# Attention and expert layer on one Trainium2 core: the batch loop in four groups of two pairs of heads, and another passage to the token tiles

## The reference

```
q = norm(x) @ Wq + bq;  k, v = ctx[:, :256] @ Wk + bk, @ Wv + bv     16 heads of 64
a = softmax(where(key > query, -1e30, q k^T / 8)) v @ Wo + bo
x = x + tanh(g_xattn) * a      (blind rows take the mean of all 1601 context rows instead)
e = argmax(norm(x) @ Wr + br)                                       one of 8 experts
x = x + tanh(g_ffn) * (relu(norm(x) @ W1[e] + b1[e]) @ W2[e] + b2[e] + what the other experts give on zero input)
```

## Time and profile before

| what | value |
|---|---|
| median of 3 executions | 360.89 us (360.82 to 364.35) |
| profiled execution, its span | 365.85 us, 363.8 us |
| granted TensorE clock, mean | 0.998 |
| PE / PEld busy | 345.6 / 283.3 us (95% / 78%) |
| DVE / ACT / POOL busy | 270.9 / 255.5 / 191.0 us (74% / 70% / 52%) |
| start and batch 0 / loop / batch 7 and tiles | 60.7 / 213.0 / 90.3 us |

### The profile page before, as it was taken

How to read it: one execution, slowest core, us unless ns; L and a number is a source line. 1 busy time by engine, 2 the same in 40 slices (tenths; PEclk the granted TensorE clock), 3 DMA queues, 4 the chain that set the end, 5 groups by cost and what they waited for, 6 DMA issues and landing times.

```text
span 363.8 us, 11160 instructions
## 1 busy us (share of the span) xinstructions
PE 345.6 (95%) x2835; PEld 283.3 (78%) x2835; DVE 270.9 (74%) x1262; ACT 255.5 (70%) x936; POOL 191.0 (52%) x369
## 2 busy tenths in 40 slices
PE   8999999999999999999999999999999897978893
PEld 6776778778878787878778877887887666968893
DVE  4789995878687868786878687867777696776671
ACT  3686775887687868785878587859773667646562
POOL 7245555366537744774467436833681570345544
PEclk9999999999999999999999999999999999999999
DMA  6999202000400030004000400040005914133320
GB/s 201 248 367 244 91 2 90 4 2 1 122 0 0 0 119 0 0 0 119 0 0 0 119 0 0 17 117 0 0 29 211 366 36 133 50 104 105 89 66 13
DMA packets 21562, 27.87 MB, mean 77 GB/s; under 512 B 3649, under 2 KB 16789, under 8 KB 21536
## 3 DMA queue, kind: packets, MB, share of 16 engines
q1 hardware_dynamic: 19776, 23.85, 21.7%
q0 software_dynamic: 1504, 3.16, 2.5%
q10 hardware_dynamic: 256, 0.56, 0.5%
HBM read 19.00 MB, written 9.01 MB: 77 GB/s over the span
## 4 chain that ended last, share of the span: by engine, by line
PE 80%; DVE 10%; issue 3%; ACT 3%; DVEq 1%; DMA 1%; another core or an unknown queue 1%; POOLq 0%; SPq 0%; POOL 0%; ACTq 0%
PE ps_kv L1255 15%; PE ps_o L1255 13%; PE ps_s L1255 13%; PE ps_t L1359 11%; PE ps_w L1255 10%; PE ps_q L1255 8%; PE ps_t L1255 7%; DVE masked L823 2%; DVE prob_T L842 2%; PE ps_s L1479 1%; ACT prob L565 1%; PE ps_w L1396 1%; DMA nat<-in_ctx 1%; DVE row_fix L830 1%
## 5 line engine op out<-in xcount | busy, mean ns | idle before, releaser
L433 POOL TENSOR_SCALAR prob<-prob,row_inv 128x128 f32<-128x128 f32 (+1 forms) x256 | 104.8, 429 | 124.9 <-DVE row_inv L836 124.7
L565 ACT ACTIVATE prob<-masked,neg_max 128x128 f32<-128x128 f32 (+1 forms) x256 | 113.7, 447 | 65.5 <-DVE neg_max L823 65.2
L823 DVE CUSTOM_DVE_ANT_0 masked<-ps_s,mask_now 128x128 f32<-128x128 f32 (+1 forms) x256 | 77.8, 353 | 44.3 <-PE ps_s L1255 40.8
L842 DVE COPY prob_T<-ps_t 128x384 f32<-128x384 f32 x123 | 65.0, 549 | 0.8 <-PE ps_t L1359 0.7
L1255 PE MATMUL ps_s<-k_T,q_T 64*128 64x128 f32 (+1 forms) x512 | 59.6, 351 | 1.5 <-DVE neg_max L823 1.5
L1359 PEld LDWEIGHTS ps_t<-ident,prob 128*128 128x128 f32 x384 | 41.0, 141 | 21.5 <-issue 17.3
L1359 PE MATMUL ps_t<-ident,prob 128*128 128x128 f32 x384 | 56.1, 282 | 0.6 <-DVE prob_T L842 0.5
L1255 PE MATMUL ps_o<-prob_T,v_nat 128*64 128x256 f32 (+1 forms) x512 | 49.8, 333 | 2.1 <-DVE prob_T L842 1.5
L565 ACT ACTIVATION_READ_ACCUMULATOR prob<-masked,neg_max 128x1 f32 x256 | 48.5, 190 | 0.0
L1255 PEld LDWEIGHTS ps_o<-prob_T,v_nat 128*64 128x64 f32 x512 | 31.7, 136 | 16.3 <-issue 2.1
L1255 PEld LDWEIGHTS ps_s<-k_T,q_T 64*128 64x128 f32 x512 | 33.9, 188 | 9.7 <-issue 6.8
(11 more groups left out here) (200 smaller groups left out, 545.9 us busy)
## 6 DMA issues: line engine op xcount, KB each, us to landing
ctx_buf<-in_ctx SPq DMA_DIRECT2D x8, 768.0 KB
sorted_rows<-pad_rows SPq DMA_DIRECT2D x8, 642.5 KB, 4.4
tile_in<-sorted_rows SPq DMA_DIRECT2D x24, 128.5 KB, 2.1
packs<-in_L_ffn_W SPq DMA_DIRECT2D x1, 2048.0 KB
packs<-in_L_ffn_W SPq DMA_DIRECT2D x8, 256.0 KB
nat<-in_ctx SPq DMA_DIRECT2D x8, 128.0 KB, 3.4
nat<-in_x SPq DMA_DIRECT2D x1, 768.0 KB, 6.6
w_in<-in_L_xattn_Wk SPq DMA_DIRECT2D x2, 256.0 KB, 4.5
```

The costliest lines, as they stand in the source:

```text
L433: g.tensor_scalar(prob[:, slot, lo:hi], prob[:, slot, lo:hi], row_inv[:, slot, t:t + 1], 1.0, ALU.mult, ALU.mult).then_inc(prob_ready, 1)
L565: s.activation(prob[:, slot, lo:hi], masked[:, slot % 2, lo:hi], ACT.Exp, bias=neg_max[:, slot, t:t + 1], scale=-1.0, accum_out=row_sum[:, ...
L823: v.tensor_tensor_reduce(out=masked[:, slot % 2, lo:hi], in0=ps_s[slot % 2][:, lo:hi], in1=mask_now[:, lo:hi], scale=-SCALE, scalar=FLOOR, ...
L842: v.tensor_copy(prob_T[:, slot % TSLOTS, :], ps_t[slot % 2][:, 0:W3]).then_inc(probT_kept, 1)
```

## The change

In the loop each batch runs in four groups g of two pairs; the four short products of a group's scores and two of its 128 by 256 ones share the two `ps_s` banks, and the other two go to `ps_kv` and `ps_q`, whose maxima are taken first (`shared_maxima`) and let the next projections start. VectorE writes into `prob` and the exponential runs in place, so `masked` goes. VectorE copies q of each odd pair, which ScalarE did. Input transpositions go to `ps_w`. In batch 0 the context's two halvings go from behind pair 0 to pairs 1 and 2, where maxima go ahead of the sums' mending. Batch 7 begins with a group's first part; its second norm for batch 6 is spread to later places, fewer weight copies stand before its last `prob_T` copy, and its last projection goes ahead of the first tile's transposition. Among the early tiles the norm's transpositions, router and ranks move, and the table's steps stand together. The diff's core, with twelve columns of indentation taken off:

```diff
             scatter(b - 1, [1])
...
-            sum_context(0)
+        if first and j == 1:
+            half_context(0)
+        if first and j == 2:
+            rest_context(0)
+def loop_batch(b):
+    for g in range(PAIRS // 2):
+        if g == 2:
+            sum_context(b + 1)
+        if g == 3:
+            residual_of(b)
+        for i in range(SUMS, SUMS + 2):
+            for h in range(2):
+                normalise(8 * b + 2 * g + i, h, (2 * (2 * g + i) + h) % SLOTS)
+            if g == 3 and i == SUMS:
+                scatter(b - 1)
...
-def exponential(p, h, slot):
+def exponential(p, h, slot, count=None):
...
     head = 2 * p + h
-    act.wait_ge(max_ready, 2 * head + 2)
-    wait(act, probT_done, head + 1 - SLOTS)
+    act.wait_ge(max_ready, 2 * head + 2 if count is None else count)
     for t, (lo, hi) in enumerate(((0, P), (P, W3))):
-        s.activation(prob[:, slot, lo:hi], masked[:, slot % 2, lo:hi], ACT.Exp,
+        s.activation(prob[:, slot, lo:hi], prob[:, slot, lo:hi], ACT.Exp,
                      bias=neg_max[:, slot, t:t + 1], scale=-1.0,
                      accum_out=row_sum[:, slot, t:t + 1]).then_inc(exp_done, 1)
...
+def loop_batch(b):
+    for g in range(PAIRS // 2):
+        j, p = 2 * g, 8 * b + 2 * g
+        a = 8 * b + PAIRS - 2 + j
+        if g == 0:
+            context_now(b + 1)
+        if g == 2:
+            keep_y(b)
+        if g == 0:
+            two_exponentials(p + SUMS, j + SUMS, 0)
+            two_exponentials(p + SUMS, j + SUMS, 1, (0,))
+        keep_q(a, a_pair(g))
+        keep_kv(a, a_pair(g))
+        if g == 1:
+            keep_mean(b)
+        if g == 2:
+            keep_x2T(b - 1)
+        if g > 0:
+            two_exponentials(p + SUMS, j + SUMS, 0)
+        else:
+            two_exponentials(p + SUMS, j + SUMS, 1, (1,))
+        keep_kv(a + 1, a_pair(g) + 1)
+        if g > 0:
+            two_exponentials(p + SUMS, j + SUMS, 1)
+        if g == 0:
+            keep_inT(b + 1)
+        for i in range(2):
+            keep_oT(b, p + i, j + i, p + 2)
...
+def masked_maximum(slot, t, scores):
+    lo, hi = ((0, P), (P, W3))[t]
+    v.tensor_tensor_reduce(out=prob[:, slot, lo:hi], in0=scores, in1=mask_now[:, lo:hi], scale=-SCALE,
+                           scalar=FLOOR, op0=ALU.add, op1=ALU.min,
+                           accum_out=neg_max[:, slot, t:t + 1]).then_inc(max_ready, 1)
 def maximum(p, h, slot):
     head = 2 * p + h
     dve.wait_ge(scores_done, p + 1)
-    wait(dve, exp_done, 2 * (head - 1))
+    wait(dve, probT_done, head + 1 - SLOTS)
     settle(dve)
     for t, (lo, hi) in enumerate(((0, P), (P, W3))):
-        v.tensor_tensor_reduce(out=masked[:, slot % 2, lo:hi], in0=ps_s[slot % 2][:, lo:hi],
-                               in1=mask_now[:, lo:hi], scale=-SCALE, scalar=FLOOR, op0=ALU.add,
-                               op1=ALU.min, accum_out=neg_max[:, slot, t:t + 1]).then_inc(max_ready, 1)
+        masked_maximum(slot, t, ps_s[slot % 2][:, lo:hi])
+def shared_maxima(p, j):
+    dve.wait_ge(scores_done, p + 2)
+    dve.wait_ge(probT_done, 2 * (p + 2) - SLOTS)
+    settle(dve)
...
+def keep_q(p, j):
+    dve.wait_ge(q_done, p + 1)
+    v.tensor_scalar(q_T[:, j, :], ps_q[:, 0:S], bias_T[:, j:j + 1], None, ALU.add).then_inc(q_dve, 1)
...
-            normalise_x(b + 1)
-        if not (last and j >= PAIRS - SUMS):
+        ahead = not (last and (j == 0 or j >= PAIRS - AHEAD)) and not (first and j == PAIRS - 1)
+        if last and j == 0:
+            shared_maxima(p + SUMS, SUMS)
+            for h in range(2):
+                own_maxima(SUMS, h)
+            short_maxima(SUMS)
+            for h in range(2):
+                keep_probT(p, h, h)
+        if first and j == 0:
+            normalise_x(1)
+        maxima_first = first and 1 <= j < 3
+        if not (last and j >= PAIRS - SUMS) and not maxima_first:
             fix_sums(p + SUMS, 2 * (j + SUMS) % SLOTS)
             invert_sums(p + SUMS, 2 * (j + SUMS) % SLOTS)
         for h in range(2):
             if ahead:
                 maximum(p + AHEAD, h, (2 * (j + AHEAD) + h) % SLOTS)
             between(b, j, h, first, last)
-        if first and j == 0:
-            normalise_x(1)
+        if maxima_first:
+            fix_sums(p + SUMS, 2 * (j + SUMS) % SLOTS)
+            invert_sums(p + SUMS, 2 * (j + SUMS) % SLOTS)
         for h in range(2):
-            if not (last and j == PAIRS - 1) and not (last and p + 1 >= SHARED and h == 1):
+            if j < PAIRS - 1 and not (last and p + 1 >= SHARED and h == 1):
                 keep_probT(p + 1, h, (2 * j + 2 + h) % SLOTS)
...
+def loop_batch(b):
+    for g in range(PAIRS // 2):
+        j, p = 2 * g, 8 * b + 2 * g
+        shared_maxima(p + SUMS, j + SUMS)
+        if g > 0:
+            for h in range(2):
+                keep_probT(p, h, (2 * j + h) % SLOTS)
+        for h in range(2):
+            own_maxima(j + SUMS, h)
+        if g == 3:
+            for step in (3, 4, 5):
+                choose(b - 1, step)
+        short_maxima(j + SUMS)
+        if g == 0:
+            normalise_x(b + 1)
+            for h in range(2):
+                keep_probT(p, h, (2 * j + h) % SLOTS)
+        for h in range(2):
+            keep_probT(p + 1, h, (2 * j + 2 + h) % SLOTS)
+        keep_q(8 * b + PAIRS - 1 + j, a_pair(g) + 1)
+        if g == 3:
+            for step in range(4):
+                place(b - 1, step)
+        fix_sums(p + SUMS, 2 * (j + SUMS) % SLOTS)
+        invert_sums(p + SUMS, 2 * (j + SUMS) % SLOTS)
+        for step in ((0, 1, 2, 3, 4), (5, 6, 7, 8, 9, 10, 11), (), ())[g]:
+            second_norm(b - 1, step)
+        if g == 2:
+            for step in range(3):
+                choose(b - 1, step)
+            dve.wait_ge(max_ready, 4 * 8 * (b + 1))
+            mask_of(b + 1)
+        if g == 3:
+            sum_context(b + 1)
+        fix_sums(p + AHEAD, 2 * (j + AHEAD) % SLOTS)
+        invert_sums(p + AHEAD, 2 * (j + AHEAD) % SLOTS)
 dve.wait_ge(ld_x[0], 16)
...
@@ -1211,23 +1344,24 @@
     second_norm(B - 1, step, ps_q)
 dve.wait_ge(rest_loaded, 16)
 early_rest(0)
-finish(0, 0)
+early_w2(5)
 dve.wait_ge(x2T_done, B)
 v.tensor_copy(x2_T[:, :], ps_w[:, S:2 * S]).then_inc(x2T_kept, 1)
+finish(0, 0)
 early_rest(1)
-finish(1, 1)
 for step in range(6):
     choose(B - 1, step)
-early_rest(2)
+finish(1, 1)
 for step in range(4):
     place(B - 1, step)
+early_rest(2)
 finish(2, 2)
-early_rest(3)
 for step in range(9):
     late_table(step)
-    if step == 3:
-        finish(3, 3)
-        early_rest(4)
+early_rest(3)
+finish(3, 3)
+early_w2(6)
+early_rest(4)
 finish(4, 4)
...
+        pe.wait_ge(x2_ready, 2 * (b - 1))
     for t in range(QT):
-        t_.transpose(ps_q[:, t * P:(t + 1) * P], x_norm[:, t, :], ident[:, :])
+        t_.transpose(ps_w[:, t * P:(t + 1) * P], x_norm[:, t, :], ident[:, :])
     for t in range(QT):
-        last = t_.transpose(ps_q[:, S + t * P:S + (t + 1) * P], ctx_now[:, t, :], ident[:, :])
+        last = t_.transpose(ps_w[:, S + t * P:S + (t + 1) * P], ctx_now[:, t, :], ident[:, :])
...
+def two_scores(p, j, b, nb, nj):
+    pe.wait_ge(k_kept, p + 2)
+    for i in range(2):
+        q_kept(b, j + i)
+    pe.wait_ge(max_ready, 4 * p)
+    for i, lo in ((0, 0), (1, W3)):
+        for h in range(2):
+            score(ps_s[h][:, lo:lo + P], j + i, h, 0)
+    for h in range(2):
+        score(ps_s[h][:, P:W3], j, h, 1)
+    pe.wait_ge(k_kept, p + 4)
+    pe.wait_ge(v_kept, p + 4)
+    q_kept(nb, nj)
+    for h in range(2):
+        score(ps_s2[h], j + 1, h, 1).then_inc(scores_done, 1)
...
 def batch(b, first=False, last=False):
+    if last:
+        for h in range(2):
+            transpose_probs(8 * b, h, h)
+        pe.wait_ge(max_ready, 4 * (8 * b + SUMS) + 1)
+        project_q(b, PAIRS - 2)
+        pe.wait_ge(max_ready, 4 * (8 * b + SUMS) + 2)
+        project_kv(b, PAIRS - 2)
     for j in range(PAIRS):
...
         if last and j == 2:
             router(b - 1)
-        if j == (0 if first else 1) and not last:
+        if first and j == 0:
             input_transposes(b + 1)
-        if j == 3 and not first and not last:
+    if last:
...
+def loop_batch(b):
+    for g in range(PAIRS // 2):
+        j, p = 2 * g, 8 * b + 2 * g
+        nb, a = (b, PAIRS - 2) if g == 0 else (b + 1, j - 2)
+        for h in range(2):
+            transpose_probs(p, h, (2 * j + h) % SLOTS)
+        if g == 2:
+            mean_through_wvo(b)
+        pe.wait_ge(max_ready, 4 * (p + SUMS) + 1)
+        project_q(nb, a)
+        pe.wait_ge(max_ready, 4 * (p + SUMS) + 2)
+        project_kv(nb, a)
+        if g == 1:
+            mean_of(b)
+        if g == 2:
             norm_transposes(b - 1, b + 1)
-        if j == 4 and not first and not last:
+        project_q(nb, a + 1)
+        for h in range(2):
+            transpose_probs(p + 1, h, (2 * j + 2 + h) % SLOTS)
+        project_kv(nb, a + 1)
+        if g == 3:
+            ranks(b - 1)
+        if g == 2:
```

(60 more changed lines are left out.)

114 lines of the change are left out of this document (69 added, 45 removed).

## The result

The changed kernel takes **360.10 us** (median of 16 executions, 359.23 to 361.86). The kernel before, now with 16 executions, has a median of 362.49 (360.82 to 364.35). The ratio is 0.9944, 95% interval 0.9927 to 0.9961: 2.0 us faster, about half a per cent. The forecast was 4.7 us. The profiled execution took 359.85 us, with a span of 358.1.

A forecast was written before the change was run, and what follows sets the result against it. TensorE's own order was taken to bound the loop. Loop -2.1, batch 0 at 0, passage and tiles -2.6 sum to -4.7 us: median 360.89 becomes 356.2, range 347.5 to 361.0.

The forecast's parts named there:

- What a switch costs: Loop, TensorE: fewer switches of array shape save 1.96 us a batch, 33.5 without waits; a double score block about 1.5.
- Rival E: Loop: a switch costs only .06, so .66 is saved against 1.61 of waits; 364.0 us in all; 5%.
- Waits that come in: Loop, TensorE: new waits of 0, .32, .76 and .53 us in the four groups, 1.61 a batch.
- The long chain: Loop, third group: exponentials, inverted sums, norm and shared maximum free `ps_q` at 9.28; TensorE, there at 8.52, waits .76.
- The loop's sum: Six loop batches: 33.5 + 1.6 = 35.1 us a batch, .36 less than before, -2.1 in all.
- Batch 0: First batch: left at 0; bounds -.9 from maxima ahead of sums, +1.0 from the half sum holding VectorE.
- Batch 7 and passage: Last batch to tile 0: fewer weight copies remove the 1.49 wait for `prob_T`; -1.9 us at the first product.
- Tile 7: Late table ready some 3.5 us earlier; tile 7 1.7 to 3.2 earlier, taken as -2.6 with the passage.
- without that cover it is .76 a copy: Weight copies moved behind the norm: free if VectorE is ahead of TensorE there, otherwise .76 us each.
- C: Rival: loop breaks even with waits of about 2 us a batch, ScalarE's 2.1 stays; 359.4 us; 18%.
- D: Rival: VectorE's port is held for GpSimd's whole run of four, slowing the norm's steps; 366 to 369 us; 8%.
- B: Rival: most loop waits are hidden, VectorE on time at the third group, .4 a batch stays; 349.3 us; 27%.

The follow-up runs named there:

- first_only: Kernel before with batch 0's new order alone (half sums behind pairs 1 and 2, maxima ahead of sums there): 362.30 us, ratio 1.0024.
- old_start: Changed kernel with batch 0's half sums and mending of sums put back in the order before the change: 360.55 us, ratio 0.9951.
- tail_only: Kernel before with only the change's weight copies, last projection, early tile order and late table: 361.52 us, ratio 0.9995.
- same_again: Kernel before, unchanged, run again for a second profiled execution: 361.54 us, ratio 1.0006.
- norm_spread: Changed kernel with the loop's second-norm steps 0 to 2 ahead of the first group's second-pair copies, only 9 to 11 in the second group: 356.13 us, ratio 0.9856.

## Why the prediction was wrong, by its own steps

- **What a switch costs: right.** A double block costs 1.51 (forecast 1.5), and transpositions behind a full-array block .66. Without its waits the batch would take 33.31 (35.56 less the 2.25 below); forecast 33.5. Some .26 of the difference to 35.45 is late products that the kernel before had (in each batch a block of transpositions of .81 and a product of q of .54, beside `in_T`), and the switches gave the other 1.9. Rival E falls.
- **Waits that come in: the place right, the size wrong, and this is what failed.** Summed over blocks against the same blocks without a wait, they are .09, .46, .89 and .81 in the four groups, 2.25 in all; the forecast had 0, .32, .76 and .53, 1.61. The long chain went as worked out: from the second group's first transposition to the pair's sums inverted 5.6 (forecast 5.67), to the norm's end 8.4 (8.24), to the product of q 9.28 (9.28). The waits themselves were .38 in the second group (forecast .32), .66 in the third (.76), .12 for the shared maximum (.23) and .43 for the values (.30) in the fourth: 1.59, as forecast in sum. In the fourth group steps 3 to 5 of the choice took 1.07 (193.29 to 194.36) and not .59, one of them .64 beside GpSimd's residual. What the walk put at nothing is the other .66. Most of it lies behind the waits: the product that starts late costs .51 to .56 and not .43, and k and v behind it .50 or .51. The walk closed the account at the first instruction, though the kernel before has such a product in every batch: q at .54 in place of .43.
- **The loop's sum: wrong in sign.** Forecast -2.1, measured +.6 (213.72 against 213.12). The margin in the forecast was a thin one: 1.96 saved, 1.61 of waits. The .64 more in the waits are 3.8 us over six batches.
- **Batch 0: forecast 0, measured -.2** for equal work, within its bounds. first_only and old_start show that the order of maxima and half sums gives nothing. Two of its score blocks are one now, worth .47 by the forecast's prices; no run tried that alone.
- **Batch 7 and passage: forecast -1.9 at the first product, measured -2.0** for equal work, and that is luck. tail_only has the forecast's own step, the copies and with them the wait of 1.49, and gives .5. Most of the rest is two waits of batch 7 that the forecast did not name. They were there before and are still in tail_only (.64 and .76), and the changed kernel has neither:

```profile
282.59 0.93 PE L1255 MATMUL ps_s<-k_T,q_T 64*128 64x128 f32 x8 [0.65 <-DVE neg_max L823]
...
285.09 0.41 PE L1396 MATMUL ps_w<-ident,rows 128*128 128x128 f32 x2 [0.77 <-ACT tg_mean L595]
```

  Whether batch 7's new beginning or the spread of its second norm took them away, no run shows.
- **Tile 7: -.7 more in the forecast, nothing measured.** The table is early, as forecast, and the wait for tile 7's rows (1.10 in same_again) goes. It is given back before: TensorE needs .6 more between the first products of tiles 1 and 2, with the norm's transpositions ahead of the second, and stands .6 at the last early product. There the sentence "without that cover it is .76 a copy" came true, for one copy (.45 of issue and .43). VectorE, after:

```profile
317.11 0.43 DVE L1128 COPY w_in<-packs 128x512 f32 x1 [0.45 <-issue]
...
317.90 0.35 DVE L1337 SCALAR_TENSOR_TENSOR tile_out<-ps_o,tg,tile_in 128x128 f32<-128x128 f32 x1
```

  The sum at 317.90 ends at 318.25 and frees the bank into which the last early product goes; that starts at 318.36.

```profile
318.36 1.13 PE L1389 MATMUL ps_o<-w_in,hidden 128*128 128x128 f32 x8 [0.42 <-issue]
```

- **The base.** The sum was made against a profiled execution of 365.85, which held 3 us that the kernel does not have as a rule. The middle value for the passage was chosen with the wait of 2.1 in mind, and the forecast subtracted from it a gain that was not there to be had.
- **The rivals.** C's loop, with waits of about 2 us a batch and no gain, is what happened, and its 359.4 lies .7 from the median; its other condition, that ScalarE's 2.1 stays, was not met, so the nearness is part luck. D falls: of seven steps beside a whole run of GpSimd none took over .58. B falls for this change, though norm_spread shows that half of the way to it was one edit off.

## What to carry to other kernels

Where a change trades switches for waits, price a wait by blocks, not by the idle time: here the one or two products behind each wait of TensorE for a product's input or bank were .1 to .25 us slower in sum, and the rows of the weight loads show it where those of the products do not. A long piece of side work belongs where its engine idles, and not between the release of one buffer and the next: moving 1.5 us of it was worth 4 us over six batches, without one instruction less. Before trusting the sum against one profiled execution, cut a second one at the same places, and count the instructions between the cuts: a block that changed sides looked like .7 us won in one stage and lost in the other.

## What was not expected of the hardware

- Waits that no row of PE names: a product of q behind a shared maximum costs .53 to .56 in place of .43, and in the fourth group PE's timeline prints no idle time at all where .30 is lost. PEld's does: the weight load waits .19, and then starts with its product and not .11 ahead of it.
- VectorE beside GpSimd is held by single instructions, not by runs: the norm's seven steps took 2.77 and not 2.27 beside four normalisations of 1.63 in all, with two steps at .58 and .54 in place of .35. This agrees with the Trainium skill ("SBUF — State Buffer", Terms), by which the port pair is held for one instruction.
- ScalarE's unexplained waits of 2.1 and 2.5 us among the tiles came in one of two executions of the same kernel; the late tiles took 38.0 to 42.0 us over eleven profiles with the same tiles in them.
